# Layer 3's attention: k and q of a head from one product, and the order of the projections

## The reference

```python
q = (x @ Wq).reshape(B, N, H, Dh).transpose(0, 2, 1, 3)
kv = x @ Wkv
k = kv[..., :H * Dh].reshape(B, N, H, Dh).transpose(0, 2, 1, 3)
v = kv[..., H * Dh:].reshape(B, N, H, Dh).transpose(0, 2, 1, 3)
s = jnp.einsum('bhid,bhjd->bhij', q * scale, k)
gm = jax.lax.stop_gradient(jnp.max(s, axis=-1, keepdims=True))
p = jnp.where(causal_mask, 0.0, jnp.exp(s - gm))
num = jnp.einsum('bhij,bhjd->bhid', p, v)
out = num / (jnp.sum(p, axis=-1, keepdims=True) + EPS)
out = out.transpose(0, 2, 1, 3).reshape(B, N, H * Dh)
return out @ Wo + bo
```

## Time and profile before

| | us |
|---|---|
| median of three runs | 2138.48 (2133.2 to 2142.51) |
| profiled execution | 2138.84 |
| its span, first to last instruction | 2135.9 |
| PE busy | 1751.4 (82%) |
| DVE busy | 1415.0 (66%) |
| ACT busy | 1224.6 (57%) |
| POOL busy | 1135.8 (53%) |
| heads of layer 3's attention | 1145 to 2070 |

### The profile page before, as it was taken

One profiled execution on the slowest core, in us unless ns is written; L12 is line 12 of the kernel. 1 busy time (PEld: TensorE's weight loads), 2 busy tenths in 40 slices (PEclk: granted clock), 3 DMA queues, 4 the chain that ended last, 5 costly groups with the idle time before them and its releaser, 6 DMA issues. The chain is left out here.

```text
span 2135.9 us, 31634 instructions
## 1 busy us (share of the span) xinstructions
PE 1751.4 (82%) x10687; PEld 1129.4 (53%) x10687; DVE 1415.0 (66%) x2084; ACT 1224.6 (57%) x2064; POOL 1135.8 (53%) x1025
## 2 busy tenths in 40 slices
PE   4737999999487477676888999899999899999958
PEld 1514777789343266443453555555555555555535
DVE  3465777763355487665238888888888888888831
ACT  4274333346246266234337877777777777777733
POOL 1154545524100366211323788888888788878860
PEclk9578999997699799797899999999999999999979
DMA  1212222221000000000413999999899998899970
GB/s 28 64 36 72 80 80 80 79 62 34 14 18 1 6 0 0 3 4 22 127 46 61 156 165 156 162 158 158 158 156 157 157 160 158 155 163 161 161 134 20
DMA packets 630961, 193.01 MB, mean 90 GB/s; under 512 B 591553, under 2 KB 622034, under 8 KB 630814
## 3 DMA queue, kind: packets, MB, share of 16 engines
q1 hardware_dynamic: 621686, 167.32, 43.4%
q0 software_dynamic: 8224, 23.51, 3.6%
q10 hardware_dynamic: 904, 0.29, 0.1%
HBM read 36.90 MB, written 12.48 MB: 23 GB/s over the span
## 5 line engine op out<-in xcount | busy, mean ns | idle before, releaser
L2833 DVE TENSOR_REDUCE half_max<-scores 128x1 f32<-128x1024 f32 x512 | 614.7, 1219 | 142.3 <-PE scores L2662 136.5
L2579 POOL TENSOR_TENSOR p_low<-p,p_high 128x2048 f16<-128x2048 f32 (+15 forms) x256 | 576.4, 2252 | 153.2 <-ACT p_high L2763 131.4
L2662 PE MATMUL scores<-k_high,q_pair 128*128 128x512 f16 x1024 | 304.1, 378 | 68.1 <-ACT p L2748 63.1
L2748 ACT ACTIVATE p<-scores,exp_bias 128x1024 f32<-128x1024 f32 (+7 forms) x384 | 317.7, 862 | 64.8 <-DVE exp_bias L2838 62.3
L2763 ACT ACTIVATE p_high<-p 128x2048 f16<-128x2048 f32 (+15 forms) x256 | 282.5, 1104 | 40.8 <-DMA pT_high<-p_high 34.1
L2662 PE MATMUL scores<-k_low,q_pair 128*128 128x512 f16 x1024 | 304.7, 379 | 0.0
L2682 PEld LDWEIGHTS scores<-v_pair,pT_high 128*128 128x128 f16 x2176 | 151.2, 99 | 108.9 <-issue 57.5
L2682 PE MATMUL scores<-v_pair,pT_low 128*128 128x129 f16 x2176 | 187.3, 223 | 15.2 <-DMA pT_low<-p_low 14.6
L2682 PE MATMUL scores<-v_pair,pT_high 128*128 128x129 f16 x2176 | 188.8, 222 | 8.5 <-DMA pT_high<-p_high 8.4
L2682 PEld LDWEIGHTS scores<-v_pair,pT_low 128*128 128x128 f16 x2176 | 147.3, 99 | 53.1 <-DMA pT_low<-p_low 21.9
L2662 PEld LDWEIGHTS scores<-k_low,q_pair 128*128 128x128 f16 x1024 | 99.3, 97 | 122.0 <-issue 0.5
(11 more groups left out here) (486 smaller groups left out, 3272.2 us busy)
## 6 DMA issues: line engine op xcount, KB each, us to landing
pT_high<-p_high SPq DMA_TRANSPOSE x256, 3.7
pT_low<-p_low SPq DMA_TRANSPOSE x256, 3.7
slots<-zero_row SPq DMA_DIRECT2D x1, 3036.0 KB, 14.3
slot_rows<-slots SPq DMA_DIRECT2D x23, 132.0 KB, 2.4
slots_out<-expert_out SPq DMA_DIRECT2D x23, 128.0 KB, 1.8
w_up<-in_L_ffn_inter_w_dram SPq DMA_DIRECT2D x1, 2048.0 KB, 9.3
dispatched<-moe_rows SPq DMA_DIRECT2D x1, 1024.0 KB
slot_rows<-dispatched SPq DMA_DIRECT2D x4, 256.0 KB, 4.0
```

The lines of the kernel that those rows point to most:

```text
L2579: pool.tensor_tensor(flat(pl[:, buf, b0:b0 + n, :]), flat(p32[:, buf, b0:b0 + n, :]), flat(ph[:, buf, b0:b0 + n, :]), ALU.subtract).then_i ...
L2662: mm = pe.matmul(ps[:, b.start + i, :], q, k[:, par, cs(2 * half + i)], start=start, stop=not start)
L2748: act.activation(flat(p32[:, buf, b0 + first:b0 + first + w, :]), flat(ps[:, banks(p, half), :])[:, 0:w * P], ACT.Exp, bias=bias[:, p:p + ...
L2833: dve.tensor_reduce(mx[:, p % 2, half:half + 1], flat(ps[:, b[half], :]), AX.X, ALU.max, negate=True)\
```

## The change

One weight tile `wkq` holds the head's 64 columns of k and of q side by side. One float32 product gives k in the lower 64 partitions and q in the upper 64, for 512 tokens. The duplication that the scores need is made by the copies out of PSUM: ACT's `high` makes three activations of 64 partitions (q's high part into both halves of `qh2`, k's into the lower half of `k2`), and DVE's `low` three subtractions of 64 partitions (q's low part into both halves of `ql2`, k's into the upper half of `k2`). The roles in the scores are exchanged: k carries high over low, q the doubled parts. Number and shape of the score matmuls stay. There are four units per head, of chunks 0, 3, 1, 2, in steps 0, 2, 4 and 6. The next head's first scores wait for all parts of all four units. SP loads two tiles per head, not four.

```diff
@@ -2410,11 +2410,10 @@
     LAG = 2
     ORDER = [NT - 1 - p // 2 if p % 2 == 0 else p // 2 for p in range(NT)]
     BLOCKS = NT + 1
-    hi = slice(DH, P)
-
-    UNITS = [("k", 0), ("k", 1), ("k", 2), ("k", 3), ("q", 0), ("q", 3), ("q", 1), ("q", 2)]
-    unit_count = lambda u: u % NCH + 1
-    assert len(UNITS) == PAIRS
+    lo, hi = slice(0, DH), slice(DH, P)
+
+    UNITS = [0, 3, 1, 2]
+    UNIT_STEP = PAIRS // len(UNITS)
     UBANK, OBANK = 6, 7
 
     RING = 3
@@ -2480,9 +2479,9 @@
         o_all = sb("o_all", [P, H // 2, NT, 2, DH])
         with ExitStack() as inner:
             sb = lambda name, shape, dt=F32: inner.enter_context(nc.sbuf_tensor(f"{name}_{nc.next_id()}", shape, dt))
-            wq, wk, wv = sb("w_q2", [P, 2, 2, DH]), sb("w_k2", [P, 2, 2, DH]), sb("w_v", [P, H * DH])
+            wkq, wv = sb("w_kq", [P, 2, 2, DH]), sb("w_v", [P, H * DH])
             v_all = o_all[:].bitcast(F16)
-            qs2, kh2, kl2 = (sb(n, [P, 2, TOK], F16) for n in ("q_pair", "k_high", "k_low"))
+            k2, qh2, ql2 = (sb(n, [P, 2, TOK], F16) for n in ("k_pair", "q_high", "q_low"))
             v2 = sb("v_pair", [P, 2, NT, VW + 1], F16)
             p32 = sb("p", [P, 2, BLOCKS, P])
             ph, pl = sb("p_high", [P, 2, BLOCKS, P], F16), sb("p_low", [P, 2, BLOCKS, P], F16)
@@ -2494,11 +2493,11 @@
...
@@ -2515,9 +2514,8 @@
                 @block.sync
                 def _(sp):
                     def load(h):
-                        for dst, src in ((wq, inp["L3_attn_Wq"]), (wk, inp["L3_attn_Wkv"])):
-                            for r in range(2):
-                                sp.dma_start(dst[:, h % 2, r, :], src[:, ds(h * DH, DH)]).then_inc((w_loaded0, w_loaded1)[h % 2], 16)
+                        for r, src in enumerate((inp["L3_attn_Wkv"], inp["L3_attn_Wq"])):
+                            sp.dma_start(wkq[:, h % 2, r, :], src[:, ds(h * DH, DH)]).then_inc((w_loaded0, w_loaded1)[h % 2], 16)
 
                     def turn_high(at, p):
                         buf, b0, n = place(p)
@@ -2543,7 +2541,7 @@
                                 turn_low(*shift(at, par, p - 1)[::2])
                             turn_high(at, p)
                             if p == 5 and not last and h + 2 < H:
-                                wait(sp, q_raw, at(NCH, NCH))
+                                wait(sp, kq_raw, at(NCH, NCH))
                                 load(h + 2)
 
                     def epilogue(at):
@@ -2630,17 +2628,15 @@
 
                     def unit_free(at, u):
 
-                        kind = UNITS[u - 1][0]
-                        wait(pe, q_low if kind == "q" else k_lows, at(NCH, unit_count((u - 1) % PAIRS), 1 if u else 0))
+                        wait(pe, q_low, at(2 * NCH, 2 * u, 1))
+                        wait(pe, k_low, at(NCH, u, 1))
 
                     def project(at, par, u, b):
 
-                        kind, c = UNITS[u]
                         if u == 0:
-                            wait(pe, (w_loaded0, w_loaded1)[par], at(32, 64 - 32 * par, 1))
-                        w, done = (wq, q_raw) if kind == "q" else (wk, k_raw)
-                        pe.matmul(ps[:, b, :], w[:, par, :, :].rearrange("p r d -> p (r d)"), m.xn[:, cs(c)],
-                                  start=True, stop=True).then_inc(done, 1)
+                            wait(pe, (w_loaded0, w_loaded1)[par], at(16, 32 - 16 * par, 1))
+                        pe.matmul(ps[:, b, :], wkq[:, par, :, :].rearrange("p r d -> p (r d)"), m.xn[:, cs(UNITS[u])],
+                                  start=True, stop=True).then_inc(kq_raw, 1)
 
                     def values(n, g, b):
 
@@ -2652,14 +2648,12 @@
                         b = banks(p, half)
                         now, par, p = shift(at, par, p)
                         if p == 0 and half == 1:
-                            wait(pe, k_lows, now(NCH, NCH))
-                            wait(pe, q_low, now(NCH, 2))
-                        if p == NT // 2 and half == 1:
-                            wait(pe, q_low, now(NCH, NCH))
-                        q = qs2[:, par, ORDER[p] * P:(ORDER[p] + 1) * P]
-                        for k, start in ((kh2, True), (kl2, False)):
+                            wait(pe, q_low, now(2 * NCH, 2 * NCH))
+                            wait(pe, k_low, now(NCH, NCH))
+                        tile = slice(ORDER[p] * P, (ORDER[p] + 1) * P)
+                        for q, start in ((qh2, True), (ql2, False)):
                             for i in range(2):
-                                mm = pe.matmul(ps[:, b.start + i, :], q, k[:, par, cs(2 * half + i)], start=start, stop=not start)
+                                mm = pe.matmul(ps[:, b.start + i, :], q[:, par, tile], k2[:, par, cs(2 * half + i)], start=start, stop=not start)
                         mm.then_inc(scored, 1)
 
                     def products(pair):
@@ -2691,9 +2685,9 @@
                                     if not (last and s == PAIRS - 1):
                                         free(at, 2 * s + 2 + i, half, first)
                                         scores(at, par, 2 * s + 2 + i, half)
-                                    if (i, half) == (0, 0) and not last:
-                                        unit_free(at, s)
-                                        project(at, 1 - par, s, UBANK)
+                                    if (i, half) == (0, 0) and s % UNIT_STEP == 0 and not last:
+                                        unit_free(at, s // UNIT_STEP)
+                                        project(at, 1 - par, s // UNIT_STEP, UBANK)
                                     if (i, half) != (0, 1) and (not first or s >= LAG):
                                         now, v_par, pair = shift(at, par, s - LAG, PAIRS)
                                         add_up(now, v_par, pair, 2 * i + 1 - half - 1, 3)
@@ -2707,7 +2701,6 @@
                         for u in range(len(UNITS)):
                             pe.wait_ge(v_low, 2 * NT - 7 + u)
                             project(at, 0, u, u % 8)
-                        pe.wait_ge(q_low, NCH)
                         for p in range(2):
                             for half in (1, 0):
                                 if (p, half) == (1, 0):
@@ -2725,13 +2718,11 @@
                 def _(act):
                     def high(at, par, u, b):
 
-                        kind, c = UNITS[u]
-                        if kind == "q":
-                            wait(act, q_raw, at(NCH, unit_count(u), 1))
-                            act.activation(qs2[:, par, cs(c)], ps[:, b, :], ACT.Copy, scale=SCALE).then_inc(q_high, 1)
-                        else:
-                            wait(act, k_raw, at(NCH, unit_count(u), 1))
-                            act.activation(kh2[:, par, cs(c)], ps[:, b, :], ACT.Copy).then_inc(k_highs, 1)
+                        here = cs(UNITS[u])
+                        wait(act, kq_raw, at(NCH, u + 1, 1))
+                        for part in (hi, lo):
+                            act.activation(qh2[part, par, here], ps[hi, b, :], ACT.Copy, scale=SCALE).then_inc(q_high, 1)
+                        act.activation(k2[lo, par, here], ps[lo, b, :], ACT.Copy).then_inc(k_high, 1)
 
                     def values_high(n, g, b):
 
@@ -2783,8 +2774,8 @@
                                     exp(at, 2 * s + 1)
                                 if not first or s + i:
                                     split(*shift(at, par, 2 * s + i - 1)[::2])
-                                if i and not last:
-                                    high(at, 1 - par, s, UBANK)
+                                if i and s % UNIT_STEP == 0 and not last:
+                                    high(at, 1 - par, s // UNIT_STEP, UBANK)
 
                     def prologue(at):
                         for u in range(2 * NT):
@@ -2807,16 +2798,13 @@
                 def _(dve):
                     def low(at, par, u, b):
 
-                        kind, c = UNITS[u]
-                        if kind == "q":
-                            wait(dve, q_high, at(NCH, unit_count(u), 1))
-                            low_part = qs2[hi, par, cs(c)]
-                            dve.scalar_tensor_tensor(out=low_part, in0=ps[hi, b, :], scalar=SCALE, in1=low_part,
+                        here = cs(UNITS[u])
+                        wait(dve, q_high, at(2 * NCH, 2 * u + 2, 1))
+                        for part in (hi, lo):
+                            dve.scalar_tensor_tensor(out=ql2[part, par, here], in0=ps[hi, b, :], scalar=SCALE, in1=qh2[hi, par, here],
                                                      op0=ALU.mult, op1=ALU.subtract).then_inc(q_low, 1)
-                        else:
-                            wait(dve, k_highs, at(NCH, unit_count(u), 1))
-                            dve.tensor_tensor(kl2[:, par, cs(c)], ps[:, b, :], kh2[:, par, cs(c)], ALU.subtract)\
-                               .then_inc(k_lows, 1)
```

(12 more changed lines are left out.)

## The result

The changed kernel takes 2308.61 us (median of four runs, 2307.05 to 2312.7) against 2138.85 us: ratio 1.081, 95% interval 1.079 to 1.083. That is slower, as forecast, but by 170 us and not by 102, and outside the range.

A forecast was written before the change was run, and what follows sets the result against it. SP's transpose queue set the head's period, with a ring of engines 2.3 us shorter. +6.6 us per head over 14 heads (92.4), +8.9 first head, -2 last, +2.5 prologue: +101.8 on 2138.8, say 2240 us; range 2186 to 2264.

The forecast's parts named there:

- The bound of the kernel before: Layer 3's attention: SP's queue of transposes sets the period of a head, 57.65 us in the fifth head.
- the ring's slack: DVE, PE and ACT wait for each other in a loop, with 2.3 us per head to spare against SP's transpose queue.
- DVE's link: Three subtractions per unit, 2.30 us, lengthen the chain in odd steps: +1.70 us replacing k's subtraction, +1.45 replacing q's.
- intervals 1, 3 and 5: Times between successive pairs' exponentials in a head, holding DVE's unit of the step before: +1.70, +1.70, +1.45 us.
- k's row, 0.60: Profiled k subtraction on DVE overlaps its neighbours and costs the chain 0.60 us; by such rows a unit adds 0.5 less.
- ACT's copies: Two more copies per unit on ACT, in steps 0, 2, 4 and 6: 0.96 us, up to 1.3 without overlap.
- the sum: Interval-by-interval addition over a head's eight steps: +6.6 us per head, a period of some 64 us, +101.8 us altogether.
- ACT's slack of 1.47 us: Step 4: ACT's idle room covers its added copies, so the interval changes by -0.6 us.
- The new wait: Step 7: the next head's first scores on PE wait for the whole unit of step 6, about 1.1 us.
- the clock: Rival, chance 0.08: PE's granted clock falls once a head, 3 us each, +45 us, giving 2285 us.
- The prologue: Before the first head: four units at 3 x 0.73 us on DVE end some 2.5 us later.
- The ends of the range: Forecast's own range: units at 1.80 us give 2221 us; copies at 1.3 in steps 0, 2, 6 give 2260.

The follow-up runs named there:

- a shorter ring: Kernel before, with DVE's subtraction moved ahead of a step's last reduction, into DVE's wait for scores: 2138.41 us, ratio 0.998.
- filled kernel: Changed kernel with 11, 10, 9 and 13 matmuls nobody reads put into PE's four longest stalls of a head: 2255.8 us.
- the same edit: Subtraction work moved ahead of a step's last reduction: changed kernel (three subtractions) 2158.58 us, kernel before (one) 2138.41 us.
- spread kernel: Changed kernel, units begun in steps 0, 2, 4, 5, the first two spread (two copies and subtractions, the third a step later): 2208.06 us.

## Why the prediction was right in sign and wrong in size

- The bound of the kernel before was read rightly: SP's queue sets the period. The loads taken off it gave 1.65 us per head, a shorter ring 4 us in all. So the ring's slack is at least 1.65 us; its 2.3 us is a reading of waits that no run measures.
- DVE's link: right. The two of q hold DVE for 1.45 us (1711.31 to 1712.76), k's for 0.72 (to 1713.48). In the filled kernel intervals 1, 3 and 5 are 1.48, 1.67 and 1.30 us longer than before; 1.70, 1.70 and 1.45 were forecast. The Trainium skill's model of held instructions (VectorE: DVE Perf Modes, "Two Vector instructions with no wait between them") said so for k's as well; k's row, 0.60, did not.
- ACT's copies: taken at 0.48 each, from the row of a full copy; they took 0.6. The timeline of ACT in step 0:

```profile
1705.88 1.21 ACT L2724 ACTIVATE q_high<-scores 64x512 f16<-64x512 f32 x2 [0.26 <-PE scores L2638]
1707.12 0.59 ACT L2725 ACTIVATE k_pair<-scores 64x512 f16<-64x512 f32 x1
1707.61 1.99 ACT L2739 ACTIVATE p<-scores,exp_bias 128x896 f32<-128x896 f32 x2
```

  From 1705.88 to 1707.61 are 1.73 us for three, where one had 0.48: 1.25 more, near the upper of the two bounds given (1.3), and 0.29 over the 0.96 of the sum. That is part of the 0.4 to 0.65 us by which intervals 0, 2 and 4 of the filled kernel exceed the forecast. In step 4 the sum also let ACT's slack of 1.47 us cover the copies; the kernel with one copy left out shows that a copy is paid there as in the other even steps.
- The new wait: right. The subtraction ends at 1762.30 (start 1761.61, 0.69 long) and PE starts at 1762.44; with the stall filled, interval 7 is 9.04 us against 9.26.

```profile
1762.44 1.01 PE L2656 MATMUL scores<-k_pair,q_high 128*128 128x512 f16 x2 [3.13 <-DVE k_pair L2807]
```

- The failed step is the clock. The sum put what longer waits do to PE at nothing: it expected one stall of PE a head, at the turn, and a granted clock of 1.0. There are four stalls, of 2.82, 2.61, 2.40 and 3.13 us, and the clock falls three times a head at some 1.3 us each, 3.9 us. The prediction named the fall as a rival, at 0.08, at 3 us once a head, and left it out of the range; with 2285 us that rival too was short. The rows to see it by stood in the sum: a unit of 2.3 us on DVE makes PE wait that much longer, in the steps 1, 3, 5 and at the head's turn, and the earlier trace rows already had a fall. The forecast of the stalls was used for DVE and ACT and not for PE.
- The prologue cost 7.6 us (first exponential at 1152.7, not 1145.1) for 2.5: DVE's four units took 8.64 us (1138.82 to 1147.46), PE stood for 7.48 and its clock was at the low level in the 6.8 us from 1144.5. Some 3.5 us of it was there before the first unit began on PE (1136.52 against 1132.99), and isn't the change's.
- The ends of the range don't follow from their terms: copies at 1.3 us in three steps add 3 x 0.34 = 1.0 us per head, where 1.3 was added, and units at 1.80 take off 4 x 0.5 = 2.0, where 1.3 was taken off without saying why. By their terms, neither end comes near 2308 us.

Sum, on the profiled executions, whose spans are 174.7 us apart where 101.8 were forecast, 72.9 missing: 57.9 are the falls (heads of the kernel after against the filled one), 9.6 what the filled kernel's heads take over the forecast, 5.1 the start (7.6 against 2.5), 0.3 the last head.

## What to carry to other kernels

In a ring of engines an instruction costs what its place leaves uncovered, not its duration: put it where its engine waits for the ring, and ask for each lump what the engines behind it will do meanwhile. PE's own idle time isn't free when it comes in one piece: here stalls of 2.6 to 3.1 us were followed by matmuls at half speed that sat on the chain. Filling the stalls gave all of that back, shortening them or moving the work most of it, filling one of four nothing. Before shortening a ring, see which queue runs level with it; here the same edit was worth 4 us on one side of that line and 150 on the other.

## What the runs showed of the hardware

- The granted clock fell to its 1.2 GHz level for 3.4 us behind stalls of PE of 2.61, 2.82 and 3.13 us, in heads where PE was busy for 53 of 68 us (78%); behind the one of 2.40 us it fell in some heads and not in others. The fall behind the stall that ended at 1717.16 began some 0.8 us after that end, so it met work that ran without a pause; a fall at 1762.3 began just before its stall ended.
- Neither the busy share of a head nor the length of one stall tells whether a fall comes. The kernel without one subtraction kept 1.00 in a head with PE busy for 48.5 of 61.6 us (79%) and stalls of up to 2.40 us (first line). The kernel before with its loads on POOL kept 1.00 through and behind a stall of 3.20 us (the other three). The spread kernel had falls behind 2.11 us. What does decide isn't settled here.

```profile
1717.50:1779.13 61.63, 48.48 (x412) 29.83 (x410) 47.27 (x59) 47.17 (x65) 47.16 (x36) 1.00 0.91 146
```

```profile
1877.90:1881.10 3.20, 0.00 (x1) 0.03 (x1) 0.44 (x1) 3.20 (x4) 1.44 (x1) 1.00 1.18 234
1881.10:1890.00 8.90, 8.63 (x71) 5.23 (x72) 6.85 (x8) 6.52 (x10) 7.79 (x6) 1.00 0.85 157
```

```profile
1881.11 0.59 PE L2669 MATMUL scores<-k_high,q_pair 128*128 128x512 f16 x2 [3.20 <-ACT p L2755]
```

The Trainium skill (TensorE: Matmul & The Clock Gate, "Part 1: The HAM clock gate") lets the level follow how busy PE has lately been. The falls here agree in so far as each followed a stall; the 3.20 us without a fall shows that the last stall alone isn't the measure.
- ACT's activations of 64 partitions that change the half they read or write take 0.59 to 0.60 us and follow each other with a gap of 0.02 to 0.03 (1705.88 to 1707.12 above, and so in all 128 places), where a full copy before overlaps the exponential behind it by 0.10 (0.58 long, 0.48 to the next start in the earlier trace rows).
